# A Perceiver block on one core: the copy of the next queries moves between the two halves of the exponentials on ScalarE

## What is computed

```python
x = x + xattn(layernorm(x), ctx, ctx)   # 16 heads of 64
x = x + retention(layernorm(x))         # 8 heads of 16, xpos, decay mask, group norm, gate
x = x + ffn(layernorm(x))               # q, k, v and f: trees of depth 8, one leaf per row
...
q = (query @ w_q).reshape(B, Q, HEADS, HEAD_DIM).transpose(0, 2, 1, 3)
k = (key @ w_k).reshape(B, Kl, HEADS, HEAD_DIM).transpose(0, 2, 1, 3)
scores = jnp.einsum('bhqd,bhkd->bhqk', q, k) * scale
attn = jax.nn.softmax(scores, axis=-1)
...
scores = jnp.einsum('bhle,bhme->bhlm', Q, K) * D[None]   # D: the decay mask
Y = jnp.einsum('bhlm,bhmv->bhlv', scores, V)
...
for _ in range(DEPTH):
    logit = jnp.einsum('bsd,bsd->bs', x, nw[node]) + nb[node]
    node = 2 * node + 1 + (logit > 0).astype(jnp.int32)
leaf = node - NN
h = act(jnp.einsum('bsd,bsdl->bsl', x, w1[leaf]) + b1[leaf])
return jnp.einsum('bsl,bsld->bsd', h, w2[leaf]) + b2[leaf]
```

## Time and profile before

| | |
|---|---|
| median of 3 runs | 669.51 us (668.91 to 670.25) |
| the profiled execution | 669.95 us |
| its span in the trace | 667.8 us |
| granted TensorE clock in it | 0.99 of full speed |
| ACT `pt_hi` copies | 256, 590 ns each |
| DVE `pt_lo` subtractions | 256, 686 ns each |
| ACT exponentials | 128, 1113 ns each |
| DVE `q_lo` subtractions | 31, 423 ns each |

### The profile page before, as it was taken

How to read it: one execution, slowest core, us unless ns; L and a number is a source line. 1 busy time by engine, 2 the same in 40 slices (tenths; PEclk the granted TensorE clock), 3 DMA queues, 4 the chain that set the end, 5 groups by cost and what they waited for, 6 DMA issues and landing times.

```text
span 667.8 us, 10976 instructions
## 1 busy us (share of the span) xinstructions
PE 622.6 (93%) x4225; PEld 536.9 (80%) x4225; DVE 452.3 (68%) x800; ACT 394.2 (59%) x836; POOL 275.8 (41%) x266
## 2 busy tenths in 40 slices
PE   7899999999999999898999999999999998878686
PEld 3688888999998989787988898778989897755564
DVE  2566656778776777777777777786777776853833
ACT  4665556677654555768565854957566755631541
POOL 3210002031110106896252447876161539864832
PEclk9999999999999999999999999999999999998998
DMA  9800000020100008040030037210210044203813
GB/s 197 229 33 1 1 1 0 1 64 32 33 1 1 1 2 306 19 131 0 1 132 1 1 116 276 72 60 1 80 52 1 6 157 168 68 1 128 342 61 130
DMA packets 21402, 48.54 MB, mean 73 GB/s; under 512 B 1508, under 2 KB 14696, under 8 KB 17256
## 3 DMA queue, kind: packets, MB, share of 16 engines
q0 software_dynamic: 4608, 34.74, 13.9%
q1 hardware_dynamic: 16168, 12.85, 7.1%
q10 hardware_dynamic: 576, 0.26, 0.2%
HBM read 47.59 MB, written 0.26 MB: 72 GB/s over the span
## 4 chain that ended last, share of the span: by engine, by line
PE 64%; POOL 13%; DVE 10%; ACT 6%; DMA 4%; issue 2%; SPq 1%; POOLq 0%; DVEq 0%; ACTq 0%
PE ps_s L434 22%; PE ps_av L434 20%; PE ps_ring L664 13%; PE ps_ring L434 4%; POOL leaf L1435 4%; PE ps_m L434 4%; ACT prob L993 2%; POOL leaf L1439 2%; DVE chunk_max L1286 2%; DVE pt_lo L1078 2%; DMA leaf<-up_v_dram,idx 2%; ACT pt_hi L924 2%; DMA leaf<-w_o_dram 2%; POOL ct_lo L1404 1%; DVE hid L1135 1%
## 5 line engine op out<-in xcount | busy, mean ns | idle before, releaser
L924 ACT CAST pt_hi<-ps_ring 128x512 fp32r<-128x512 f32 x256 | 144.5, 590 | 147.8 <-PE ps_ring L664 147.5
L1078 DVE TENSOR_TENSOR pt_lo<-ps_ring,pt_hi 128x512 fp32r<-128x512 f32 x256 | 170.3, 686 | 64.0 <-ACT pt_hi L924 63.9
L993 ACT ACTIVATE prob<-ps_s,neg_max 128x1024 f32<-128x1024 f32 x128 | 141.6, 1113 | 27.2 <-DVE neg_max L1369 27.1
L664 PE MATMUL ps_ring<-ident,prob 128*128 128x128 f32 x1024 | 145.0, 274 | 12.1 <-DVE q_lo L1078 4.9
L1286 DVE TENSOR_REDUCE chunk_max<-ps_s 128x1 f32<-128x1024 f32 x128 | 150.5, 1215 | 5.3 <-PE ps_s L434 5.1
L434 PE MATMUL ps_av<-pt_hi,c_hi 128*128 128x256 f32 x512 | 151.2, 295 | 0.0
L664 PEld LDWEIGHTS ps_ring<-ident,prob 128*128 128x128 f32 x1024 | 116.9, 141 | 39.3 <-issue 18.9
L434 PE MATMUL ps_av<-pt_lo,c_hi 128*128 128x256 f32 x512 | 144.7, 283 | 0.0
L434 PE MATMUL ps_av<-pt_hi,c_lo 128*128 128x256 f32 x512 | 144.7, 283 | 0.0
L434 PE MATMUL ps_s<-ct_hi,q_hi 128*128 128x512 f32 x256 | 112.5, 440 | 3.9 <-ACT prob L993 1.8
L434 PE MATMUL ps_s<-ct_hi,q_lo 128*128 128x512 f32 x256 | 101.4, 396 | 0.0
(11 more groups left out here) (267 smaller groups left out, 765.3 us busy)
## 6 DMA issues: line engine op xcount, KB each, us to landing
stage<-ctx_t_dram SPq DMA_DIRECT2D x16, 256.0 KB, 3.4
stage<-ctx_rows_dram SPq DMA_DIRECT2D x16, 256.0 KB, 2.9
leaf<-w_v_dram SPq DMA_DIRECT2D x1, 512.0 KB, 8.0
leaf<-w_o_dram SPq DMA_DIRECT2D x1, 512.0 KB, 10.2
dec<-decay_dram SPq DMA_DIRECT2D x1, 512.0 KB
nw<-node_w_dram SPq DMA_DIRECT2D x1, 510.0 KB
wsm<-w_small_dram SPq DMA_DIRECT2D x1, 448.0 KB
leaf<-wq_t_dram SPq DMA_DIRECT2D x1, 384.0 KB, 11.6
```

What stands on the lines that cost most here:

```text
L664: last = nc.tensor.transpose(o[:, i * P:(i + 1) * P], prob[:, n % 2, k:k + P], ident[:])
L924: nc.scalar.copy(pt_hi[:, pp, row:row + KPC, P * (n % 2):P * (n % 2 + 1)], ps_ring[:, i % 2, :].rearrange("p (k q) -> p k q", k=KPC)).then ...
L993: nc.scalar.activation(prob[:, n % 2, 1024 * e:1024 * (e + 1)], ps_s[:, 1024 * e:1024 * (e + 1)], ACT.Exp, bias=neg_max[:, n:n + 1], accum ...
L1078: return nc.vector.tensor_tensor(o, a, b_, op)
```

## The change

ACT's exponentials are put into a function for one half. The copy of X now stands between the two calls. Nothing else is touched: the same instructions run on each engine, with the same semaphores.

```diff
+            def exponential(n, e):
+
+                nc.scalar.activation(prob[:, n % 2, 1024 * e:1024 * (e + 1)], ps_s[:, 1024 * e:1024 * (e + 1)], ACT.Exp,
+                                     bias=neg_max[:, n:n + 1], accum_out=sums[:, n, e:e + 1]).then_inc(S["exp_done"], 1)
+
...
                 if 0 <= n < HEADS:
                     act.wait_ge(S["negmax_ready"], n + 1)
-                    for e in range(2):
-                        nc.scalar.activation(prob[:, n % 2, 1024 * e:1024 * (e + 1)],
-                                             ps_s[:, 1024 * e:1024 * (e + 1)], ACT.Exp,
-                                             bias=neg_max[:, n:n + 1], accum_out=sums[:, n, e:e + 1])\
-                            .then_inc(S["exp_done"], 1)
+                    exponential(n, 0)
                 if s and (query_pair(s - 1) is not None or wqk_pair(s - 1) is not None):
                     i = RING[("X", s - 1, 0)]
                     act.wait_ge(S["ring_filled"], i + 1)
...
                         wqk_scaled(2 * wqk_pair(s - 1), 2, ps_ring[:, i % 2, 2 * P:4 * P]).then_inc(S["ring_taken"], 1)
+                if 0 <= n < HEADS:
+                    exponential(n, 1)
                 if s % 2 and 5 <= s < HEADS:
                     take_context((s - 5) // 2)
```

## The result

The changed kernel takes 674.66 us (median of 5, 673.3 to 676.08) against 669.51 us: 0.8% slower, ratio 1.0077 (1.005 to 1.0104). The forecast was 672.2 and slower; the sign is right, but the loss is 5.2 us where 2.7 were forecast, and the time lies above the range.

The account below looks back on a forecast made before the run. PE was taken as the bound up to slot 23, with 29% of the chain on POOL, DVE and ACT. −0.93 + 1.77 + 1.77 + 0.12 = +2.73 on the profiled 669.95, with the median 0.44 lower, gave 672.2 us; range 668.6 to 673.8.

Parts of the forecast that it names:

- the ordinary slot: In each ordinary odd slot the copy still waits for its product; first `pt_hi` comes 1.09 us later, second `pt_lo` 0.59.
- The wait of 37.5 us: ACT's wait for the X product ahead of `q_hi`, forecast to grow from 8.4 to some 40 us.
- the choice: Slots 29, 45 and 61, the values' leaf choice: `hit` and POOL's `idx` come 0.59 us later each time, +1.77 in all.
- the decay product: Slots 23, 39 and 55: DVE's second decay product, which PE multiplies by, starts 0.59 us later each time, +1.77 in all.
- slot 3: The product is ready early there, so `q_hi` moves earlier and PE's 0.93 us wait for `q_lo` goes: −0.93, bounds 0 and −1.06.
- the stalls that aren't kept: Slots 31, 47, 35 and 51: PE's waits for `q_lo` (0.54, 0.55, 0.94 each) give way to POOL's work; nothing gained.
- About two of the seven waits: Sign of being right: PE's waits for `q_lo`, 4.9 us in all, fall from seven times to about two.
- The rule on breaking up instructions: Skill rule speaking for the change: by it alone PE's 4.9 us of waits would come back, giving 664.6 us.
- The +0.12 of slots 41 and 57: The gelu table load stands behind the second `pt_hi`, which is 0.05 to 0.06 us later there: +0.12.
- in most of the slots the shift costs nothing: DVE's 0.59 us shift is covered by ACT's `pt_hi` copies waiting for PE's transposes, 147.5 us in 126 places.

## Why the prediction was partly right

**Right: the ordinary slot.** The copy waits for its product, `pt_hi` is 1.09 later, the second `pt_lo` 0.59. The wait of 37.5 us was put at about 40.

**Right: the choice.** +1.77 was forecast; the table gives 0.57, 0.56 and 0.58.

**Wrong in size: the step "It will start 0.59 later, three times: 3 × 0.59 = +1.77" on the decay product.** The delay itself was right (0.58), but its price was taken as the delay alone. It measured 2.2, 0.6 and 2.2, together 5.0: in two of three places the clock fell for 3.4 us behind the wait. The trace of before gave no sign of this: it has the sixteen products without a wait ahead of them, and waits of 0.5 to 1.3 us with other work behind them, and its clock is 1.00 at both. It never has the two together. The forecast took over that a wait costs its length, and its range had no room for a wait that costs more than that. In three kernels the wait was left in place: it brought a fall in 2, 2 and 3 of 3 slots. In the kernel before, and in the eight other kernels without it, there was none in these slots.

**Right: slot 3, and the stalls that aren't kept.** Slot 3's 0.93 came out as 1.06 to 1.09 in the traces without a fall of the clock near it. In slots 31, 35, 47 and 51 PE's waits for `q_lo` went and nothing was gained: the distance in the table is the same at 31 and 37 (3.20, 3.18). (About two of the seven waits were expected to stay waits for `q_lo`; none did.) PE and POOL in slot 35 of the changed kernel, in the place of the earlier trace rows:

```profile
316.19 1.22 PE L664 MATMUL ps_ring<-ident,prob 128*128 128x128 f32 x8
318.28 0.36 PE L434 MATMUL ps_av<-pt_hi,c_hi 128*128 128x256 f32 x1 [0.88 <-issue]
```

```profile
315.68 5.01 POOL L1414 TENSOR_TENSOR c_lo<-stage,c_hi 128x512 fp32r<-128x512 f32 x4
```

The context product comes 0.88 of idle after the transposes, where it had none: the wait has moved from `q_lo` to POOL's `c_lo`, which ends two of its pieces at 315.68 + 5.01 / 2 = 318.19. The rule on breaking up instructions (the Trainium skill, "Perfetto Trace Analysis", Optimizing Scalar/DVE Operations) says "may", and the trace agrees for one of the seven waits, slot 3's. The others were not what the end of the kernel waited for. In slots 33 and 49 PE even stands still about as long as before, 0.48 and 0.46 us at the same transposes, now for ACT's exponentials.

**Small misses.** The +0.12 of slots 41 and 57 didn't come (0.00 at slot 41). The 0.43 between slots 17 and 21 was not counted; where "in most of the slots the shift costs nothing", slots 18 and 19 were exceptions. The two traces show most of it: in slot 18 DVE comes to `x_sb`, which frees T1's bank, without the 0.27 us of idle time that it had before, and T1 starts 0.45 us behind the start of its forerunner instead of 0.24; in slot 19 T2 and T3 take 1.21 us together instead of 1.04. No run tried this.

**The sum again**, from the changed kernel's trace: between slots 9 and 63 it loses 0.43 + 5.0 + 1.71 + 0.2 = 7.34. At slot 9 it is 1.83 ahead of the kernel before, of which slot 3 explains 1.06 and the rest is left open, and behind slot 63 it loses 0.34 more: 7.34 − 1.83 + 0.34 = 5.85, the difference of the two profiled executions (675.80 − 669.95). The medians show 5.2.

Left open: whether the new order in slots 1 to 3 gains anything that a median can show. Beside the choice moved ahead it stands at 0.9912 of the kernel before against 0.9895 without it, but the two were measured on different chips, and the intervals overlap.

## What to carry to other kernels

Where PE is about to wait, price the wait together with what the clock does after it: here 0.6 us of lateness on DVE cost 2.2 in two places of three. If a producer must be late, let its reader on PE stand behind some other work that is ready, or give PE something to do: either took the fall away. And before a copy is moved ahead of a long instruction, look at whether it waits for its engine or for its input: in 22 of 31 slots the input was the one that came last, and then the move only delays what stands behind it. The chain in order of time also names what is worth moving: its row `hit` → `idx` pointed at a step that could be taken 3 us earlier for nothing, and was worth 1%.

## What was not expected of the hardware

The clock fell to its lower level after a wait as short as 0.42 us, followed by sixteen products of 128x16. Neither part brought a fall alone. The same sixteen products without the wait brought none in nine kernels (27 slots), and neither did they with two products of 128x512 in its place. The kernel before has 14 waits of 0.47 to 1.35 us between 230 and 563 us with other work behind them, and no fall among them. Each of the seven falls in these slots lost about the same, 1.7 us, whether the wait was 0.42 or 0.55. Whether a wait of 0.42 brought one varied from slot to slot and from execution to execution (4 of 6); of those of 0.55, all three did.

Five more falls lie between slots 9 and 64 of the traces, all in kernels with the late choice and all behind a longer wait of PE: of the twelve waits of 1.81 to 1.98 us around slots 31, 47 and 63 in the four kernels with the new order in slots 29, 45 and 61 and the choice of the leaf where it was, five were followed by one; of the fifteen of 1.26 to 1.45 in the five kernels with the old order there, none. These falls cost 0.2 us at most in the table.
